# Delta rule with VectorE block transposes, eight slots to a loop turn, and a head start on the output projection

## The chip, the cores and the metric

The kernel runs on one core of one Trainium2 chip. The metric is the time of one execution on the device, in microseconds (us). TensorE, VectorE (DVE), ScalarE (ACT), GpSimd (POOL) and SyncE (SP) work through their own instruction streams and meet at semaphores.

## The reference

One decoder layer on x of 4 sequences by 512 tokens by 512 features, in float32:

```
x = x + attn(layernorm(x))      # gated delta rule, 16 key heads, 32 value heads of 128
x = x + xattn(layernorm(x), ctx)
x = x + ffn(layernorm(x))
```

The change touches the first line only. Its attention is

```
mixed = silu(causal_conv(h @ w_qkv, 4 taps)); q, k, v = split(mixed); q, k = l2norm(q), l2norm(k)
per token: S = S*exp(g); delta = (v - k.S)*beta; S = S + k x delta; o = q.S
core = rmsnorm(o) * norm_weight * silu(h @ w_z);  out = core @ w_out      # 4096 -> 512
```

## The kernel before

A first stage writes the normalized x, turned, into SBUF (`xT`, 128 x 4 x 2048). `delta_rule` then goes through 64 units, one for each of 16 key heads (with its two value heads) and 4 sequences. `tail` does the output projection, the cross attention and the feed-forward part.

The delta rule is a pipeline of **slots**. Slot n projects and prepares unit n (`project`), inverts the triangular matrices of unit n-1 (`invert`) and runs the recurrence of unit n-2 (`recur`), in four chunks of 128 tokens. Each engine has its own order of the pieces of a slot, written out by hand in a function `slot` in its block, and every engine works strictly in that order. `slots` unrolls the first `ROUND` = 4 slots, then a hardware loop (`Fori(1, ROUNDS, 1)`, 15 turns of 4 slots) runs the bulk, and two further slots drain the pipeline: slot 64 with invert and recur, slot 65 with recur alone. In the trace, line 618 is the projection (`tile(n, j)`, 4 matrix products of 128x512 f32, each of which is two MATMUL records), six of them to a slot.

**The inversion.** For each of 2 heads and 4 chunks a 128x128 unit triangular matrix is inverted by doubling, in float16. The blocks grow from 2x2 (`LEVELS` = 6 levels, block half `2 << l`). Two copies are kept: `dm`, the inverse so far, and `em`, its transpose. A level l makes z = (B times even columns of dm), masked by VectorE into `zm` (line 923); d = em times zm, which VectorE adds into `dm` (line 927); and e = zm times odd columns of em, which VectorE adds into `em` (line 933). On TensorE these are `level_z` (line 688), `level_d` (697) and `level_e` (708), 8 products of 128x64 f16 each. `em` starts as the masked matrix plus identity, made by GpSimd (`e_masked`, line 538, `e_first`, line 544). Its transpose is made by TensorE (`turn_e0`, line 677, products with a float16 identity, 4 for each head) and copied by ScalarE (`copy_d0`, line 1128).

**The recurrence** is a chain through all four engines: `solve` (747), ScalarE copies `uu` (1144), `grow` (755), `attend` (766), VectorE updates the state (957), `read_k` (730), VectorE makes the residual (947), `solve` again. At its end GpSimd scales the outputs (564, 566, 573), TensorE turns them (`o_turn`, 772), VectorE gates them (`gated`, 973), and SP stores them to `core_rows` in HBM.

**The tail** opens with the output projection: for each of 16 token tiles, 32 products of 128x512 f32 (`project_out`, line 1384), one for each value head, accumulated in four PSUM banks `acc`. The core comes back from HBM in pieces of four heads by four tiles (1 MB, SP queue, line 1315), the weights `wout` in four pieces of 2, 6, 12 and 12 heads, all issued at once from ScalarE's queue (line 1825).

Of the kernel before, what the change touches and what calls it, by code (L numbers as in the profile page):

```python
# [23 lines left out]
ROUND = 4  # L24
# [11 lines left out]
HC = FF // P  # L36

# [254 lines left out]
def delta_rule(nc, xT, tabs, cons, nw, decay_dram, w_dram, core_dram):  # L292

    with ExitStack() as ctx:
# [19 lines left out]
        id16 = sb("id16", [P, P], F16)  # L314
# [3 lines left out]
        junk = sb("junk", [P, 4 * NC, P], BF16)  # L318
# [3 lines left out]
        ring = [ctx.enter_context(nc.psum_tensor(f"d_ring{i}", [P, S], F32)) for i in range(RING)]  # L322
        tz, td, te = (ctx.enter_context(nc.psum_tensor(f"d_{n}", [P, S], F32)) for n in ("tz", "td", "te"))
# [12 lines left out]
        e0_ready, a_done, d0_ready = sem("e0_ready"), sem("a_done"), sem("d0_ready")  # L336
# [7 lines left out]
        def slots(eng, slot):  # L344

            for r in range(ROUND):
                slot((0, r), True, r >= 1, r >= 2)
            with eng.Fori(1, ROUNDS, 1) as q:
                for r in range(ROUND):
                    slot((q, r), True, True, True)  # L350
            slot((ROUNDS, 0), False, True, True)
            slot((ROUNDS, 1), False, False, True)

# [40 lines left out]
        def per_token(ap):  # L394
# [5 lines left out]
        RING_ORDER = ("k", "q", "v1", "k_turn", "v0_turn", "z1", "khat_turn",  # L400
                      "v1_turn", "kk", "kq", "v0", "z0", "q_turn")
        RING_BANK = {"k": 1, "q": 0, "v1": 2, "k_turn": 1, "v0_turn": 0, "z1": 0, "khat_turn": 0, "v1_turn": 1, "kk": 0, "kq": 2, "v0": 1, "z0": 2, "q_turn": 0}
        RING_FREED = {"k": (taps, "taps", 2), "q": (taps, "taps", 5), "v0": (taps, "taps", 8), "v1": (taps, "taps", 11),
                      "z0": (z_silued, "z_silued", 0), "z1": (z_silued, "z_silued", 1),
                      "k_turn": (khat_ready, "once", 0), "khat_turn": (kT_ready, "once", 0), "q_turn": (q_squares, "squares", NC - 1),
                      "kk": (bf_ready, "bf_ready", 1), "kq": (p_ready, "p_ready", 0),
                      "v0_turn": (vn_ready, "vn_ready", 0), "v1_turn": (vn_ready, "vn_ready", 1)}
        CONV_ORDER = ("k", "q", "v1", "v0")
        CONV_BUFFER = {name: i % 2 for i, name in enumerate(CONV_ORDER)}
        SILUED = {"k": (silued, "silued", 0), "q": (silued, "silued", 1), "v0": (silued, "silued", 2), "v1": (silued, "silued", 3)}  # L410
        POSITION = {"once": (1,), "squares": (1, 2, 3, 4), "projected": (1, 2, 4, 3), "tap0": (1, 2, 4, 3), "silued": (1, 2, 4, 3),
                    "taps": (1, 2, 3, 4, 5, 6, 10, 11, 12, 7, 8, 9), "e0_ready": (3, 1, 4, 2), "z_projected": (2, 1),
                    "z_silued": (2, 1), "gam_ready": (1, 2), "gamc_ready": (1, 2), "gams_ready": (2, 1), "ks_ready": (2, 1),
                    "bf_ready": (1, 2), "bh_ready": (2, 1), "bl_ready": (1, 2), "p_ready": (2, 1), "v_turned": (1, 2),
                    "vn_ready": (1, 2), "a_done": (2, 1), "d0_ready": (2, 1), "refined": (1, 2), "zr_ready": (1, 2),
                    "closed": (1, 2), "tt_ready": (2, 1), "o_turned": (1, 2), "core_ready": (1, 2)}
        LAGGED = ("z0", "z1", "kq", "v0_turn", "v1_turn")
# [8 lines left out]
        def free(eng, n, name, order, place, freed):  # L426

            slot_, v = back(n, -(name in LAGGED)), order.index(name)
            for _ in range(3 * len(order)):
# [4 lines left out]
                unit = back(slot_, order[v] in LAGGED)  # L434
# [6 lines left out]
        def _(sp):  # L441
# [12 lines left out]
            for j in (0, TILES, 1, 3, 2, 5, 4):  # L454
                load_weights(0, j)
# [33 lines left out]
            for r in range(ROUND):  # L489
                slot((ROUNDS - 1, r), True, True, True)  # L490
            slot((ROUNDS, 0), False, True, True)
            slot((ROUNDS, 1), False, False, True)
# [3 lines left out]
        def _(pool):  # L496

            nc.gpsimd.tensor_copy(id16[:, :], cons[:, C_ID:C_ID + P]).then_inc(ids_ready, 1)
# [10 lines left out]
            def k_norm(n):  # L509
# [3 lines left out]
                wait(pool, khat_ready, count(n, 1))  # L513
# [35 lines left out]

            def decayed_keys(m, h):  # L550
                pool.wait_ge(khat_ready, count(m))
                nc.gpsimd.tensor_tensor(by_chunk(ks_[m[1] % 2][h]), by_chunk(khat[m[1] % 2]), per_token(tab(m, Q_BEND, h)),
                                        ALU.mult).then_inc(ks_ready, 1)
# [21 lines left out]
            def slot(n, project, invert, recur):  # L575
# [4 lines left out]
                if invert:  # L580
                    decayed_keys(m, 1)
                    decayed_keys(m, 0)
                if project:
# [4 lines left out]
                if invert:  # L588
                    i_minus_d(m, 0)
                if recur:  # L590
                    o_norm(s)
                    o_scale(s)
                if invert:
                    i_minus_d(m, 1)
                if project:
                    e_masked(n, 1)
                    e_first(n, 1)
                    q_norm(n)
                    e_masked(n, 0)
                    e_first(n, 0)  # L600
                    b_low(n, 0)
                    b_low(n, 1)

# [3 lines left out]
        def _(pe):  # L607
            def ring_free(n, name):
                free(pe, n, name, RING_ORDER, RING_BANK, RING_FREED)
# [27 lines left out]
            def khat_turn(n):  # L637
                pe.wait_ge(khat_ready, count(n))
# [29 lines left out]
            def turn_e0(m, h):  # L668
                if first(m):
                    pe.wait_ge(ids_ready, 1)  # L670
                pe.wait_ge(e0_ready, nth(m, "e0_ready", GV + h))
                if h == 0:
                    wait(pe, tt_ready, nth(m, "tt_ready", 1, 1))
                else:
                    wait(pe, zr_ready, nth(m, "zr_ready", 1, 1))
                for c in range(NC):
                    last = nc.tensor.matmul(chunk((tz, td)[h], c), piece(em[m[1] % 2], h, c), id16[:, :], start=True, stop=True)
                last.then_inc(a_done, 1)

            def level_z(m, l):  # L680
                if l == 0:
                    pe.wait_ge(d0_ready, at(m, GV, GV))
# [9 lines left out]
            def level_d(m, l):  # L692
                pe.wait_ge(z_ready, at(m, LEVELS, l + 1))
                if l:
                    pe.wait_ge(e_added, at(m, LEVELS, l))
# [5 lines left out]
            def level_e(m, l):  # L701
                pe.wait_ge(z_ready, at(m, LEVELS, l + 1))
                if l:
                    pe.wait_ge(e_added, at(m, LEVELS, l))
                else:
                    wait(pe, tt_ready, nth(m, "tt_ready", 0, 1))
# [14 lines left out]
            def close(m, h):  # L721
                pe.wait_ge(zr_ready, nth(m, "zr_ready", 0) if h == 0 else at(m, GV, GV))
                pe.wait_ge(e_added, at(m, LEVELS, LEVELS))
# [3 lines left out]

            def read_k(s, c):
                pe.wait_ge(s_ready, at(s, 6, 2 * c))
                nc.tensor.matmul(psa[:, 0:GV * P], chunk(kT[s[1] % 4], c), state[:, :], start=True, stop=True).then_inc(ks_s, 1)  # L730

            def read_q(s, c):
                pe.wait_ge(s_ready, at(s, 6, 2 * c))
                pe.wait_ge(o_ready, at(s, NC, c))
# [39 lines left out]

            def slot(n, project, invert, recur):
                m, s = back(n, 1), back(n, 2)
                if invert:
                    turn_e0(m, 1)
                if project:
                    tile(n, 0)  # L780
                if recur:
                    solve(s, 0)
                if invert:
                    turn_e0(m, 0)
                if project:
                    tile(n, 1)
                if invert:
                    level_z(m, 0)
                if recur:
                    grow(s, 0)  # L790
                    attend(s, 0)
                if invert:
                    level_d(m, 0)
                    level_e(m, 0)
                if recur:
                    read_k(s, 1)
                if project:
                    tile(n, 3)
                if invert:
                    level_z(m, 1)  # L800
                if recur:
                    solve(s, 1)
                    read_q(s, 1)
                if project:
                    k_turn(n)
                if invert:
# [1168 lines left out]
```

## Time and profile before

| | |
|---|---|
| median of 3 runs | 3666.68 us (3666.51 to 3670.01) |
| the profiled execution | 3667.28 us, of which the span of the trace is 3665.5 us |
| TensorE busy, mean granted clock | 3487.7 us (95%), 0.977 |
| VectorE, ScalarE, GpSimd busy | 2314.8 (63%), 1369.4 (37%), 1520.7 us (41%) |
| delta rule, from its first product to the last store | about 105 to 2806 us |
| tail | about 2806 us to the end |

The span is cut by stages: what holds in one does not hold in another. In the timeline a row is start, duration, engine, line, operation, output and inputs, shape, count, and in brackets the idle time of the engine before it with what ended it. TensorE's products are pipelined: a product's duration includes its latency, so costs on TensorE are read from the distance between starts.

### The profile page before, as it was taken

The page shows a single profiled execution, that of the slowest core. Times are in us where ns is not written, and L with a number is a line of the kernel's source. Part 1 is how long each engine was busy: PE and PEld are TensorE (multiplying, and loading weights), DVE is VectorE, ACT ScalarE, POOL GpSimd, SP SyncE. Part 2 cuts the span into 40 slices and gives each one's busy share as a digit, 9 for nine tenths or more (in the row PEclk, how much of TensorE's full clock was granted, in tenths as well). Part 3 has the DMA queues.
Part 4 walks back from the last instruction along what each step waited for, and adds up shares of the span by engine and source line. Part 5 has one row for each costly group of instructions (what it writes and reads, how often), then busy time and mean ns, then how long its engine had stood idle before and what let it go on. Part 6 is the DMA issues. An engine that isn't in the chain of part 4 may idle for free. (4 is left out here: it accounts for less than half of the span.)

```text
span 3665.5 us, 67720 instructions
## 1 busy us (share of the span) xinstructions
PE 3487.7 (95%) x23472; PEld 2207.6 (60%) x23472; DVE 2314.8 (63%) x4006; ACT 1369.4 (37%) x4187; POOL 1520.7 (41%) x1473
## 2 busy tenths in 40 slices
PE   4799999999999999999999999999996999999999
PEld 4466666666666666666666666666664444455444
DVE  4587777877778777878778777778772000014453
ACT  1344444444444444444444444444441000011232
POOL 0455554555545455555554555545551000001032
PEclk7999999999999999999999999999997999999999
DMA  1111111111111111111121111111104232311001
GB/s 55 44 36 30 42 42 37 30 36 44 34 36 30 36 32 51 30 36 36 31 48 30 36 30 41 43 37 30 36 24 157 87 115 69 103 58 69 1 9 38
DMA packets 94404, 165.88 MB, mean 45 GB/s; under 512 B 7841, under 2 KB 40737, under 8 KB 92449
## 3 DMA queue, kind: packets, MB, share of 16 engines
q1 hardware_dynamic: 93440, 152.47, 14.4%
q10 hardware_dynamic: 576, 8.39, 0.6%
q8 instruction: 225, 3.69, 0.4%
q14 instruction: 163, 1.33, 0.1%
HBM read 122.83 MB, written 38.01 MB: 44 GB/s over the span
## 5 line engine op out<-in xcount | busy, mean ns | idle before, releaser
L618 PE MATMUL d_ring<-xT,d_w 128*128 128x512 f32 x3072 | 1424.5, 607 | 12.0 <-DMA d_w<-in_w 11.6
L618 PEld LDWEIGHTS d_ring<-xT,d_w 128*128 128x128 f32 x3072 | 574.7, 194 | 585.6 <-issue 567.2
L890 DVE SCALAR_TENSOR_TENSOR d_conv<-d_ring,d_w,d_conv 128x511 f32<-128x511 f32 (+2 forms) x768 | 570.7, 743 | 287.2 <-ACT d_conv L1082 282.4
L1384 PE MATMUL t_acc<-t_area 128*128 128x512 f32 x1024 | 444.8, 595 | 18.4 <-DMA t_area<-core_rows 18.4
L1082 ACT ACTIVATE d_conv<-d_ring,d_w 128x512 f32<-128x512 f32 x256 | 176.5, 689 | 599.3 <-PE d_ring L618 599.3
L1384 PEld LDWEIGHTS t_acc<-t_area 128*128 128x128 f32 x1024 | 194.5, 191 | 256.7 <-issue 237.9
L923 DVE TENSOR_TENSOR d_zm<-d_tz,cons 128x512 f16<-128x512 f32 x384 | 264.2, 688 | 118.9 <-PE d_tz L688 114.5
L559 POOL TENSOR_TENSOR d_imd<-cons,d_dm 128x512 f16<-128x512 f32 x128 | 148.4, 1160 | 434.5 <-ACT d_dm L1133 434.5
L1613 DVE TENSOR_TENSOR t_x<-t_acc,t_x 128x512 f32<-128x512 f32 x16 | 11.1, 692 | 419.5 <-PE t_acc L1384 419.5
L511 POOL TENSOR_TENSOR d_rkt<-d_kss,cons 128x4 f32<-128x4 f32 x64 | 12.9, 201 | 610.9 <-ACT d_junk L1100 610.9
L933 DVE TENSOR_TENSOR d_em<-d_te,d_em 128x512 f16<-128x512 f32 x384 | 262.1, 683 | 4.5 <-PE d_td L697 0.2
L1873 POOL TENSOR_SCALAR t_veps<-t_mv 128x1 f32<-128x1 f32 x32 | 9.7, 303 | 575.1 <-DVE t_mv L1623 575.1
L927 DVE TENSOR_TENSOR d_dm<-d_td,d_dm 128x512 f16<-128x512 f32 x256 | 175.7, 686 | 71.6 <-PE d_td L697 71.6
L1144 ACT ACTIVATE d_uu<-d_psa 128x256 f32<-128x256 f32 x256 | 98.2, 384 | 276.9 <-PE d_psa L747 276.9
L688 PEld LDWEIGHTS d_tz<-d_dm,d_bh 128*128 128x128 f16 x3072 | 138.5, 98 | 93.0 <-issue 72.1
L1148 ACT ACTIVATE d_junk<-d_oo 128x128 bf16<-128x128 f32 x512 | 154.8, 302 | 100.6 <-DVE d_oo L967 98.1
L544 POOL TENSOR_TENSOR d_em<-d_em,cons 128x512 f16<-128x512 f16 x128 | 186.9, 1460 | 10.0
L899 DVE TENSOR_TENSOR_SCAN d_gam<-d_decay,d_ident 128x512 f32<-128x512 f32 x128 | 170.2, 1330 | 24.9 <-issue 22.0
L520 POOL TENSOR_TENSOR d_gamc<-d_gam,d_tabm 128x512 f32<-128x512 f32 x128 | 164.0, 1282 | 20.5 <-POOL d_tabm L507 13.7
L1775 ACT ACTIVATE t_xT<-t_turn 128x512 f32<-128x512 f32 x32 | 18.2, 596 | 397.2 <-PE t_turn L1367 397.2
L766 PE MATMUL d_psb<-d_uu,d_pT 128*128 128x128 f32 x1024 | 162.8, 282 | 0.6 <-ACT d_uu L1144 0.5
L525 POOL TENSOR_TENSOR d_gam<-d_gamc,cons 128x512 f32<-128x512 f32 x128 | 159.9, 1271 | 5.0
(223 smaller groups left out, 6791.1 us busy)
## 6 DMA issues: line engine op xcount, KB each, us to landing
d_decay<-decay_rows SPq DMA_DIRECT2D x64, 512.0 KB, 6.1
core_rows<-d_core SPq DMA_DIRECT2D x64, 512.0 KB, 3.3
t_area<-core_rows SPq DMA_DIRECT2D x32, 1024.0 KB, 5.5
d_w<-in_w SPq DMA_DIRECT2D x96, 256.0 KB, 2.8
t_area<-in_wout ACTq DMA_DIRECT2D x2, 3072.0 KB, 21.3
ln_x<-in_x SPq DMA_DIRECT2D x16, 256.0 KB, 5.1
t_x<-in_x SPq DMA_DIRECT2D x4, 1024.0 KB, 9.9
t_area<-in_ctx SPq DMA_DIRECT2D x4, 1024.0 KB, 7.5
```

The source lines that it names most:

```text
L520: nc.gpsimd.tensor_tensor(by_chunk(gamc[n[1] % 2][h]), by_chunk(gam[h]), per_token(tab(n, Q_BETA, h)), ALU.mult).then_inc(gamc_ready, 1)
L525: nc.gpsimd.tensor_tensor(by_chunk(gam[h]), by_chunk(gamc[n[1] % 2][h]), bc(cons[:, C_LT:C_LT + P], NC), ALU.mult).then_inc(gams_ready, 1)
L544: nc.gpsimd.tensor_tensor(e0, e0, bc(cons[:, C_ID:C_ID + P], NC), ALU.add).then_inc(e0_ready, 1)
L618: last = nc.tensor.matmul(bank(TILE[j])[:, :], wtile(j, k), xT[:, k, r % B * S:(r % B + 1) * S], start=k == 0, stop=k == KT - 1)
L766: last = nc.tensor.matmul(chunk(psb, h), chunk(pT[s[1] % 2][h], c), chunk(uu, h), start=True, stop=True)
L890: nc.vector.scalar_tensor_tensor(c[:, d:S], bank(TILE[j])[:, 0:S - d], tap(j, KS - 1 - d), c[:, d:S], ALU.mult, ALU.add).then_inc(taps, 1)
L899: nc.vector.tensor_tensor_scan(gam[h][:, :], decay[r % 2][:, h, :], ident[:, :], 0.0, ALU.mult, ALU.add).then_inc(gam_ready, 1)
L923: nc.vector.tensor_tensor(even(zm[l], l), packed(tz, l), bc(mask, GV * NC), ALU.mult).then_inc(z_ready, 1)
L927: nc.vector.tensor_tensor(even(dm, l), packed(td, l), even(dm, l), ALU.add).then_inc(d_added, 1)
L933: nc.vector.tensor_tensor(odd(e, l), packed(te, l), odd(e, l), ALU.add).then_inc(e_added, 1)
L1082: nc.scalar.activation(conv_of(TILE[j])[:, :], bank(TILE[j])[:, :], ACT.Copy, scale=tap(j, KS - 1)).then_inc(tap0, 1)
L1384: return nc.tensor.matmul(acc[t][:, :], core[(grp * CHUNKS + q) % 3][:, t, h * P:(h + 1) * P], w[:, head, :], start=head == 0, stop=head = ...
```

## The change

1. `turn_e0` and `copy_d0` go. VectorE makes the transpose itself: `flip_e0` transposes `em` in 32x32 blocks into `dm` (one instruction, 128x1024 f16).
2. `level_e` goes for levels 0 to 3 on TensorE and VectorE. `flip_d(m, l)` transposes `dm` back into `em` in 32x32 blocks after each `level_d` of levels 0 to 3 (up to level 3 nothing lies outside diagonal blocks of 32). Levels 4 and 5 stay as they were, `level_d` of level 5 and `level_e` of 4 and 5 on TensorE.
3. `normal_k`, `first_state` and the first `output` move from VectorE to ScalarE. `p_full`, twice a slot, moves from VectorE to GpSimd, which can't read PSUM, so ScalarE copies the product first (`copy_kq`).
4. The order of the pieces of a slot is new on all four engines, and so are the banks and buffers given to them.
5. `ROUND` goes from 4 to 8: 8 slots unrolled ahead, 7 turns of 8 slots.
6. During slots 64 and 65 SP loads the cores of heads 0 to 7 of the first sequence and their weights into `xT` (4 transfers of 1 MB). 24 of the output projection's products are spread over slot 65 on TensorE, between the steps of the recurrence. The tail does the other 8 of these first, starts its own loads at head 8, and issues the second to fourth piece of weights one by one, each when a piece of the core has landed.

```diff
-ROUND = 4
+ROUND = 8
+EARLY = 24
...
-            def turn_e0(m, h):
...
-                    last = nc.tensor.matmul(chunk((tz, td)[h], c), piece(em[m[1] % 2], h, c), id16[:, :], start=True, stop=True)
...
+            def flip_e0(m):
+                dve.wait_ge(e0_ready, at(m, 2 * GV, 2 * GV))
+                nc.vector.transpose(dm[:, :], em[m[1] % 2][:, :]).then_inc(flipped, 1)
+
+            def flip_d(m, l):
+                dve.wait_ge(d_added, at(m, 4, l + 1))
+                nc.vector.transpose(em[m[1] % 2][:, :], dm[:, :]).then_inc(flipped, 1)
...
+            def p_full(m, h):
+                pool.wait_ge(kqs_ready, count(m))
+                pool.wait_ge(gamc_ready, nth(m, "gamc_ready", h))
+                nc.gpsimd.tensor_tensor(pT[m[1] % 2][h][:, :], kqs[:, :], gamc[m[1] % 2][h][:, :], ALU.mult).then_inc(p_ready, 1)
...
+            def head_start(n, i):
+                if isinstance(n[0], int) and n == (ROUNDS, 1):
+                    if i == 0:
+                        pe.wait_ge(early[0], 48)
+                        pe.wait_ge(vn_ready, GV * ITERS)
+                        pe.wait_ge(z_silued, GV * ITERS)
+                        pe.wait_ge(zr_ready, GV * ITERS)
+                    for piece in range(EARLY * i // 19, EARLY * (i + 1) // 19):
+                        if piece == 4 * KT:
+                            pe.wait_ge(early[1], 16)
+                        early_product(nc, acc, xT, piece)
...
+            sp.wait_ge(z_projected, GV * (ITERS - 1))
+            sp.wait_ge(stored, 16 * (ITERS - 4))
+            for q, b in ((0, 1), (1, 0)):
+                sp.dma_start(xT[:, :, b * S:(b + 1) * S], core_rows[0:NC, :, q * S:(q + 1) * S].rearrange("t p n -> p t n")).then_inc(early[0], 16)
+            sp.dma_start(xT[:, :, 2 * S:3 * S], wout[:, 0:KT, :]).then_inc(early[0], 16)
...
-        PARTS = (0, 2, 8, 20, HV)
+        PARTS = (8, 12, 16, 24, HV)
...
+            for piece in range(EARLY, 8 * KT):
+                early_product(nc, acc, xT, piece)
...
             for i in range(4):
+                if i:
+                    act.wait_ge(core_loaded[i - 1], 16)
```

The new order on TensorE in one slot (n: project, m: invert, s: recur; `flip` stands for the VectorE transpose that it waits for):

```
tile(n,0) | z0 (after flip_e0) | solve0 | kq | d0 | grow0 attend0 | z1 | read_k1 | tile(n,1) | solve1 |
d1 (after flip_d 0) | k_turn | read_q1 grow1 | z2 | tile(m,5) | d2 | attend1 read_k2 | khat_turn | z3 |
read_q2 solve2 | kk | grow2 | d3 | tile(n,2) | z4 | attend2 read_k3 | d4 e4 | read_q3 | q_turn | solve3 |
z5 | v_turn1 | attend3 | d5 e5 | tile(n,3) | refine x2 | tile(m,4) | close0 | o_turn x2 | close1 | v_turn0
```

VectorE's new slot begins `flip_e0, decays, level_z(0), convolve, level_d(0), convolve, level_z(1)`.

## Rows read from the trace of the kernel before

**Rows 1.** Windows: a steady slot; the last slot with the drain after it.

```profile
core 0: us, PE busy (x) PEld busy (x) DVE busy (x) ACT busy (x) POOL busy (x), PEclk, DMA share, GB/s
1125.30:1165.43 40.13, 40.13 (x327) 27.53 (x325) 32.13 (x57) 19.36 (x64) 22.42 (x21) 1.00 0.11 32
...
2778.20:2806.50 28.30, 15.19 (x64) 10.64 (x64) 7.51 (x19) 6.07 (x26) 3.73 (x3) 0.73 0.11 38
```

**Rows 2.** Timeline of TensorE: first products of slots 1, 2 and 64.

```profile
134.44 0.38 PE L677 MATMUL d_td<-d_id,d_em 128*128 128x128 f16 x4 [3.43 <-POOL d_em L544]
...
170.48 0.39 PE L677 MATMUL d_td<-d_id,d_em 128*128 128x128 f16 x4
...
2744.18 0.39 PE L677 MATMUL d_td<-d_id,d_em 128*128 128x128 f16 x4
```

**Rows 3.** Timeline of TensorE: removed pieces and what starts behind them.

```profile
1007.56 0.40 PE L708 MATMUL d_te<-d_em,d_zm 128*128 128x64 f16 x8
1007.80 0.68 PE L730 MATMUL d_psa<-d_state,d_kT 128*128 128x256 f32 x2
...
1042.53 0.39 PE L677 MATMUL d_tz<-d_id,d_em 128*128 128x128 f16 x4
1042.76 2.79 PE L618 MATMUL d_ring<-xT,d_w 128*128 128x512 f32 x6
```

**Rows 4.** Timeline of TensorE: the start of a loop turn.

```profile
1082.15 0.60 PE L677 MATMUL d_td<-d_id,d_em 128*128 128x128 f16 x4 [3.48 <-POOL d_em L544]
1082.55 6.48 PE L618 MATMUL d_ring<-xT,d_w 128*128 128x512 f32 x8
1088.87 0.61 PE L747 MATMUL d_psa<-d_vn,d_tt 128*128 128x128 f32 x4
```

**Rows 5.** Groups of instructions by line and shape: VectorE.

```profile
L933 DVE TENSOR_TENSOR d_em<-d_te,d_em 128x512 f16<-128x512 f32 x384 | 262.1, 683 | 4.5 <-PE d_td L697 0.2
...
L952 DVE COPY d_state<-d_psa 128x256 f32<-128x256 f32 x64 | 26.5, 415 | 2.5 <-PE d_psa L755 2.5
...
L1685 DVE SCALAR_TENSOR_TENSOR t_area<-t_area,t_thr 128x1024 f16<-128x1024 f32 x1 | 1.3, 1285 | 0.0
...
L1684 DVE TENSOR_SCALAR t_area<-t_area,t_nthr 128x1024 f16<-128x1024 f32 x1 | 0.8, 755 | 0.0
...
L899 DVE TENSOR_TENSOR_SCAN d_gam<-d_decay,d_ident 128x512 f32<-128x512 f32 x128 | 170.2, 1330 | 24.9 <-issue 22.0 <-DMA d_decay<-decay_rows 2.9
...
L263 DVE RECIPROCAL gt_be<-gt_w 128x512 f32<-128x512 f32 x1 | 3.4, 3354 | 0.0
```

**Rows 6.** Groups of instructions by line: GpSimd and ScalarE.

```profile
L525 POOL TENSOR_TENSOR d_gam<-d_gamc,cons 128x512 f32<-128x512 f32 x128 | 159.9, 1271 | 5.0
...
L1137 ACT ACTIVATE d_oq<-d_psb,d_tabm 128x128 f32<-128x128 f32 x384 | 118.8, 362 | 15.4 <-PE d_psb L735 15.2
...
L1128 ACT ACTIVATE d_dm<-d_td 128x512 f16<-128x512 f32 x64 | 38.2, 597 | 49.7 <-PE d_td L677 49.7
```

**Rows 7.** Timelines of TensorE and VectorE: from level_z to level_d of level 0.

```profile
1006.11 0.40 PE L688 MATMUL d_tz<-d_dm,d_bh 128*128 128x64 f16 x8
...
1007.32 0.40 PE L697 MATMUL d_td<-d_zm,d_em 128*128 128x64 f16 x8
...
1006.55 0.69 DVE L923 TENSOR_TENSOR d_zm<-d_tz,cons 128x512 f16<-128x512 f32 x1 [0.95 <-PE d_tz L688]
```

**Rows 8.** Timeline of TensorE: slot 65 and the first product of the tail.

```profile
2779.10 0.71 PE L747 MATMUL d_psa<-d_vn,d_tt 128*128 128x128 f32 x4 [2.11 <-DVE d_tt L943]
...
2794.21 0.71 PE L766 MATMUL d_psb<-d_uu,d_pT 128*128 128x128 f32 x4 [0.47 <-ACT d_uu L1144]
2800.43 1.12 PE L772 MATMUL d_psa<-cons,d_oo 128*128 128x128 f32 x4 [5.50 <-POOL d_oo L573]
...
2820.79 9.52 PE L1384 MATMUL t_acc<-t_area 128*128 128x512 f32 x16 [18.40 <-DMA t_area<-core_rows]
```

**Rows 9.** The chain that ended last, in order of time: start, us, what.

```profile
2806.53 14.22 DMA t_area<-core_rows
2820.79 30.12 PE t_acc L1384 x64
...
2865.98 96.14 PE t_acc L1384 x224
```

More of the change, by code:

```diff
@@ L352, in slots, with long_slots @@
             slot((ROUNDS, 1), False, False, True)
+        def long_slots(eng, slot):
+            for r in range(ROUND):
+                slot((0, r), True, r >= 1, r >= 2, r >= 3)
+            with eng.Fori(1, ROUNDS, 1) as q:
+                for r in range(ROUND):
+                    slot((q, r), True, True, True, True)
+            slot((ROUNDS, 0), False, True, True, True)
+            slot((ROUNDS, 1), False, False, True, True)
+            slot((ROUNDS, 2), False, False, False, True)
         def count(n, before=0):
@@ L666, in _ @@
             PIECES = [(h, c) for h in range(GV) for c in range(NC)]
-            def turn_e0(m, h):
[L669 to L676, printed above, removed]
-                    last = nc.tensor.matmul(chunk((tz, td)[h], c), piece(em[m[1] % 2], h, c), id16[:, :], start=True, stop=True)
-                last.then_inc(a_done, 1)
             def level_z(m, l):
                 if l == 0:
-                    pe.wait_ge(d0_ready, at(m, GV, GV))
+                    pe.wait_ge(flipped, at(m, 5, 1))
+                    wait(pe, tt_ready, nth(m, "tt_ready", 1, 1))
                 elif l < 5:
@@ L693, in level_d @@
                 pe.wait_ge(z_ready, at(m, LEVELS, l + 1))
[L694 to L695 removed]
+                if l == 0:
+                    wait(pe, zr_ready, nth(m, "zr_ready", 1, 1))
+                elif l < 5:
+                    pe.wait_ge(flipped, at(m, 5, l + 1))
+                else:
+                    pe.wait_ge(e_added, at(m, 2, 1))
                 for h, c in PIECES:
@@ L789, in slot @@
                 if recur:
+                    solve(s, 0)
+                    head_start(n, 0)
+                if invert:
+                    kq(m)
+                    level_d(m, 0)
+                if recur:
                     grow(s, 0)
+                    head_start(n, 1)
                     attend(s, 0)
[L792 to L798, printed above, removed]
+                    head_start(n, 2)
                 if invert:
@@ L871, in slot @@
                 if recur:
+                    solve(s, 3)
+                    head_start(n, 15)
+                if invert:
+                    level_z(m, 5)
+                    v_turn(m, 1)
+                if recur:
+                    attend(s, 3)
+                    head_start(n, 16)
+                if invert:
+                    level_d(m, 5)
+                    level_e(m, 5)
+                if project:
+                    tile(n, 3)
+                if invert:
+                    refine(m, 1)
+                    refine(m, 0)
+                    tile(m, 4)
+                    close(m, 0)
+                if recur:
+                    o_turn(s, 0)
+                    head_start(n, 17)
                     o_turn(s, 1)
+                    head_start(n, 18)
                 if invert:
-                    close(m, 0)
                     close(m, 1)
+                    v_turn(m, 0)
             slots(pe, slot)
```

461 lines of the change are left out of this document (233 added, 228 removed).

## The prediction, made before the changed kernel ran

> **What bounds the kernel now.** I read the table of engines first (TensorE busy 95%), then cut the span into stretches. In a steady slot TensorE is busy for all 40.13 us, at full clock [rows 1]. VectorE is busy for 32.1 of them, GpSimd for 22.4, ScalarE for 19.4. So in the delta rule TensorE's own work is the time. A cut there counts whole, and work put on the others is free as long as they keep up. Three things are not steady. At the back edge of the loop TensorE idles 3.5 us and its next eight products take 6.48 us [rows 4]. The last slot is a chain of small steps with TensorE busy for 15.2 of 28.3 us and a granted clock of 0.73 [rows 1]. The tail opens with 14.2 us of waiting for transfers [rows 9]. Behind that the chain that ended last is nearly all TensorE again.
>
> **Removed from TensorE.** A `level_e` holds it for 1007.80 - 1007.56 = 0.24 us, a `turn_e0` for 1042.76 - 1042.53 = 0.23 us [rows 3]. The other removed ones differ by 0.01. Four of the first and two of the second make 1.39 us a slot, for 64 slots with inversion 89.0 us. The steady slot goes from 40.14 to 38.75 us if nothing new holds TensorE up.
>
> **Do the others keep up?** VectorE loses four `level_e`, two `p_full` and `normal_k`, all of the 128x512 form at 0.683 us, and two copies of 0.415 us [rows 5]: 5.61 us. It gains five block transposes of 128x1024 f16. The trace shows none. From below: the 128x1024 operation in the fastest mode seen takes 0.755 us; from above: a scan of 512 takes 1.33, so 2.66 us for 1024 [rows 5]. I take 1.285 us, the row of one element at a time over the same 1024 elements. Then VectorE has 32.1 - 5.6 + 6.4 = 32.9 us in a slot of 38.75, 85%. With the lower bound it has 30.3, with the upper 39.8 us. The Trainium skill (VectorE: DVE Perf Modes, The three transpose paths) gives 311 ns for 128x128 bf16 in 32x32 blocks. An estimate from it, 896 further elements at its 0.96 GHz, is 1.24 us each and would leave the sum where it is; no row here shows a transpose.
>
> GpSimd gains two `p_full`, at 1.27 us as its nearest row [rows 6]: 22.4 + 2.5 = 25.0 us. ScalarE loses two copies of 0.597, gains one of them back as `copy_kq`, four of 128x128 at 0.362 for `normal_k` and two of 128x256, at most 0.6 each [rows 6]: 19.4 + 2.1 = 21.5 us. Both have room.
>
> Totals don't show waits inside the slot, so I walked through the new order by hand. From the start of `level_z` to that of `level_d` at least 1.21 us pass (products, 0.44 to the mask, 0.69 the mask) [rows 7]. In the new order `solve0` and `kq` stand between z0 and d0, about 0.9 us, and 0.24 of z0: a hole of 0.07. Between d0 and z1 stand `grow0` and `attend0`, about 1 us, while VectorE puts a tap of the convolution ahead of the addition: a hole of 0.1 to 0.2. Everywhere else a projection tile (3.4 us) or several small pieces cover the flip and the addition. `flip_e0` runs under `tile(n,0)` with about 1 us to spare; if it is late, z0 is, and with it the whole level 0. I put 0.2 us a slot: +12.8 us, with bounds of 0 and 0.5 (0 and 32 us).
>
> **The loop.** From slot 2 to slot 64 are 62 slots, 2573.7 us [rows 2], 85.3 more than 62 times 40.135. There are 14 back edges, so one costs 6.1 us: about 3.3 idle and 2.8 for products at half clock (6.48 where 3.65 is usual) [rows 4]. With eight slots there are 6 back edges: 8 times 6.1 = -48.8 us. At a turn TensorE now meets a tile first, but the idle stretch is its own restart, and I leave its price.
>
> **The start.** In slot 0 TensorE waited 3.43 us for GpSimd's `em` [rows 2]. Now `tile(1,0)` stands in front of the first use: -3.4 us.
>
> **Slots 64 and 65 and the opening of the tail.** A product of the output projection costs 96.14 / 112 = 0.86 us (224 records, two each) [rows 9]. 24 of them leave the tail: -20.6 us. The tail's first load wait, 14.2 us [rows 9], is filled by the 8 further products, 6.9 us at full clock and some 2.8 more if the clock has dropped, while 2 MB come in instead of all pieces at once: -14.2 us. In exchange slot 65 fills up. From `solve0` to `attend3` it took 2794.21 - 2779.10 = 15.1 us [rows 8]. There are 20 products in that stretch now, 17.2 us, beside 7.5 us of its own products at full clock (0.43 to 0.52 each). One or two products cover each step of ScalarE or VectorE, so it is their sum, 24.7: +9.6 us. The 5.5 us for GpSimd before `o_turn` [rows 8] stay, and the last four products lie under it and under the store. I add 2.8 us for one more half-clock stretch, as a turn of the loop shows. Together -22.4 us. The early loads wait in SP's queue ahead of the store of slot 64. What they wait for (projections and older stores) is long done, or, for the last one, done some microseconds before, and no compute waits behind them. In slot 64 with few tiles the chain of levels sets the time, and two VectorE steps of a level (1.3 us) become three (2.6 us), one of them beside the products: +1.5 us.
>
> **Sum**, against the profiled execution's 3667.28 us (0.6 above the median): 3667.3 - 89.0 + 12.8 - 48.8 - 3.4 - 22.4 + 1.5 = 3518 us. With no holes and no half clock in slot 65 it is 3501, with 0.5 us of holes 3537.
>
> **Rivals.**
> (a) *The flips are as dear as a scan.* At 2.66 us VectorE has 39.8 us of work a slot and becomes the bound; slots of 39.8 to 40.3 us instead of 38.95 give 3572 to 3604 us. For it: an instruction no row prices. Against: it has one input and no carried sum.
> (b) *A turn costs in proportion to its body.* 6 turns of 12.2 instead of 6.1 us: 3518 + 36.6 = 3555 us. For it: the body to fetch is twice as long. Against: once restarted, no stretch of a slot shows TensorE short of instructions.
> (c) *VectorE and GpSimd block each other.* A scan beside GpSimd takes 1.33 us in the mean, and GpSimd now reads SBUF for two more instructions. If each flip waits half of a 1.27 us instruction in the 64% of the time that GpSimd works, VectorE has 2 us more, 35 of 38.75, and the two tight places grow by some 0.6 us: +38 us, 3556 us. The Trainium skill (SBUF — State Buffer, Who interferes with whom) says that the two share one port pair, taken by a VectorE instruction with two SBUF inputs or in a two-port mode, and not by one with a single input outside these. By it a flip would stay clear unless it runs in a two-port mode; the trace can't say.
> (d) *The head start is void*: early data come late or the drain grows by as much as the tail loses. 3518 + 22 = 3540 us.
> (e) *Slower than before.* Outside the steady slot the change wins about 70 us, 1.1 us a slot. The slot must exceed 41.2 us for a loss, so flips must exceed (41.2 - 26.5) / 5 = 2.9 us. At the reciprocal's rate, 3.354 us for 512 elements [rows 5], 6.7 each, a slot would take 60 us and the kernel 3667 + 64 x 19.9 - 70 = 4870; at 3.5 us, 44.0 and 3844 us.
>
> **How the numbers follow.** The forecast 0.66, (a) 0.10, (b) 0.10, (c) 0.06, (d) 0.05, (e) 0.03. The range 3490 to 3580 holds the forecast, (b), (c), (d) and the cheap end of (a). The forecast's own is 3497 to 3540. A difference of over 0.2%, 7 us, is what can be told here: all but (e) are faster, and a little is kept for a dear flip between (a) and (e): faster 0.95, same 0.01, slower 0.04.
>
> **What would show it.** Flips of 1.1 to 1.4 us; steady slots of 38.75 to 39.3 us with TensorE busy throughout; 6 stretches of about 3.3 us idle with a half-clock tile behind; `solve0` to `attend3` of slot 65 in 25 to 28 us; no wait over 2 us in the tail's first 50 us. It is wrong if VectorE is busy over 95% in a slot, if TensorE waits on `flipped`, or if a turn costs over 9 us.

## The result, and the profile after

The changed kernel takes 3484.94 us (median of 4 runs, 3484.55 to 3488.6) where the kernel before takes 3667.24 on the same chip: a ratio of 0.9504, with a 95% interval from 0.9487 to 0.952. The gain is 182 us. I had forecast 149 and put the time between 3490 and 3580, so the sign and most of the mechanism came out and the size did not: the result lies 5 us under the range. The profiled execution of the change took 3488.6 us, with a span of 3485.6, against 3665.5 before.

The page of the changed kernel: the table of engines, then one group of instructions (busy us, mean ns of one, idle before).

```profile
PE 3369.7 (97%) x20912; PEld 2098.0 (60%) x20912; DVE 2352.2 (67%) x3750; ACT 1447.7 (42%) x4507; POOL 1646.7 (47%) x1600
...
L958 DVE STREAM_TRANSPOSE d_em<-d_dm 128x1024 f16<-128x1024 f16 x256 | 317.5, 1240 | 4.4
```

A flip takes 1.24 us. The windows of the changed kernel answer to [rows 1], first a steady slot, then from the first solve of slot 65 to the first product of the tail.

```profile
1071.12:1109.83 38.71, 38.71 (x291) 26.00 (x287) 32.88 (x52) 20.54 (x68) 24.38 (x23) 1.00 0.09 29
2624.40:2662.38 37.98, 31.72 (x112) 18.29 (x112) 5.82 (x15) 6.50 (x28) 3.73 (x3) 0.91 0.17 56
```

TensorE is still busy for the whole of a slot at full clock, and VectorE for 32.9 us of it (the forecast had 32.9). TensorE remains the bound, and what was cut from it counts whole. The drain of slot 65 has TensorE busy for 31.7 of 38.0 us.

The start of a turn on TensorE, which answers to [rows 4], and then on VectorE:

```profile
1024.00 0.61 PE L650 MATMUL acc<-cons,d_vraw 128*128 128x128 f32 x4
1027.08 5.39 PE L644 MATMUL acc<-xT,d_w 128*128 128x512 f32 x8 [2.48 <-issue]
```

```profile
1025.02 0.68 DVE L985 TENSOR_TENSOR d_tt<-d_tz,d_em 128x512 f32<-128x512 f32 x1
1027.52 1.25 DVE L954 STREAM_TRANSPOSE d_dm<-d_em 128x1024 f16<-128x1024 f16 x1 [1.82 <-issue]
```

TensorE idles 2.48 us here, and its tile runs in 5.39 us. At two of the six turns it idles 1.90 us and the tile takes 3.69, the time at full clock; these turns cost 2.1 us each. At the other four it idles 2.13 to 2.52, the granted clock is at half for part of the tile, which takes 5.39, and they cost 4.1 to 4.4. Before it idled 2.92 to 3.60 us.

The tail's opening on TensorE, which answers to the load wait of [rows 9]:

```profile
2654.54 1.12 PE L801 MATMUL d_psa<-cons,d_oo 128*128 128x128 f32 x4 [4.35 <-POOL d_oo L596]
...
2662.42 8.80 PE L1290 MATMUL acc<-xT 128*128 128x512 f32 x16 [1.96 <-PEq L295]
2671.06 19.48 PE L1452 MATMUL acc<-t_area 128*128 128x512 f32 x45
```

The eight further products take 8.80 us, and the first product that needs the large load starts right behind them, without a wait.

**Where the 180 us of span went**, by the time of the first solve of each slot:

| stretch | forecast | measured |
|---|---|---|
| start to the first solve of slot 2 | -4.6 (-3.4 for the wait, -1.2 for slot 1) | +1.8 |
| steady slots between 2 and 63 (61 of them) | -72 | -91 |
| turns of the loop in the same stretch | -49 | -63 |
| slots 63 and 64 | -1 | -2 |
| slot 65 and the tail | -22.4 | -25.2 (+10.6 and -35.8) |

A steady slot went from 40.14 us to 38.57 or 38.64, with 38.89 in every eighth. Fourteen turns cost 6.0 us each beyond a steady slot (84 us in all), six turns now cost 3.6 each (21 us). In the last row the first number runs from the first solve of slot 65 to the start of the tail (before 2806.5, in the change 2662.4), the second from there to the end.

### The profile page after: what moved, and what is told of

It reads as the page before. It is cut to its first block and busy times, and to the rows that moved or that the text cites. A ratio compares the mean times of both kernels' runs of the same rounds, so it can differ in the third digit from the quotient of the medians.

```text
span 3485.6 us, 61745 instructions
## 1 busy us (share of the span) xinstructions
PE 3369.7 (97%) x20912; PEld 2098.0 (60%) x20912; DVE 2352.2 (67%) x3750; ACT 1447.7 (42%) x4507; POOL 1646.7 (47%) x1600
## 5 line engine op out<-in xcount | busy, mean ns | idle before, releaser
L644 PE MATMUL acc<-xT,d_w 128*128 128x512 f32 x3072 | 1412.8, 603 | 25.4 <-issue 13.2
L644 PEld LDWEIGHTS acc<-xT,d_w 128*128 128x128 f32 x3072 | 563.1, 192 | 589.8 <-issue 573.9
L935 DVE SCALAR_TENSOR_TENSOR d_conv<-acc,d_w,d_conv 128x511 f32<-128x511 f32 (+2 forms) x768 | 570.2, 742 | 22.3 <-ACT d_conv L1114 16.1
L1452 PE MATMUL acc<-t_area 128*128 128x512 f32 x768 | 332.4, 592 | 0.0
L958 DVE STREAM_TRANSPOSE d_em<-d_dm 128x1024 f16<-128x1024 f16 x256 | 317.5, 1240 | 4.4
L1114 ACT ACTIVATE d_conv<-acc,d_w 128x512 f32<-128x512 f32 x256 | 177.6, 694 | 289.6 <-PE acc L644 289.6
L969 DVE TENSOR_TENSOR d_dm<-acc,d_dm 128x512 f16<-128x512 f32 x256 | 176.6, 690 | 105.1 <-PE acc L716 104.4
L550 POOL TENSOR_TENSOR d_bl<-d_bf,d_bh 128x512 f16<-128x512 f32 x128 | 148.1, 1157 | 167.9 <-ACT d_bh L1154 167.9
L571 POOL TENSOR_TENSOR d_pT<-d_kqs,d_gamc 128x512 f32<-128x512 f32 x128 | 163.0, 1274 | 5.4 <-ACT d_kqs L1170 5.4
L703 PE MATMUL d_tz<-d_dm,d_bh 128*128 128x64 f16 x3072 | 153.1, 193 | 6.6 <-DVE d_dm L954 4.4
```

Source lines behind the costliest of these rows:

```text
L571: nc.gpsimd.tensor_tensor(pT[m[1] % 2][h][:, :], kqs[:, :], gamc[m[1] % 2][h][:, :], ALU.mult).then_inc(p_ready, 1)
L644: last = nc.tensor.matmul(bank(TILE[j])[:, :], wtile(j, k), xT[:, k, r % B * S:(r % B + 1) * S], start=k == 0, stop=k == KT - 1)
L703: last = nc.tensor.matmul(packed(tz, l, (h * NC + c) * HALF, HALF), chunk(bh[m[1] % 2][h], c), even(dm, l, (h * NC + c) * P, P), start=Tru ...
L935: nc.vector.scalar_tensor_tensor(c[:, d:S], bank(TILE[j])[:, 0:S - d], tap(j, KS - 1 - d), c[:, d:S], ALU.mult, ALU.add).then_inc(taps, 1)
L958: nc.vector.transpose(em[m[1] % 2][:, :], dm[:, :]).then_inc(flipped, 1)
L969: nc.vector.tensor_tensor(even(dm, l), packed(td, l), even(dm, l), ALU.add).then_inc(d_added, 1)
```

## The experiments

Thirteen kernels ran, each beside the kernel before. "The change" is the changed kernel. Where slots are given, they are from one first solve to the next in that kernel's own trace, and the cost of a turn is what a turn takes beyond steady slots. Not all ran on the same chip, so a few us between two of them are read from the ratios too.

**1. Eight slots to a turn, nothing else.**

```
-ROUND = 4        (kernel before)
+ROUND = 8
```

> The kernel before with eight slots to a turn of the loop and nothing else changed (6 back edges for 14). Theory Q (what a turn costs hangs on how much work TensorE still has queued behind its last wait when the loop turns; the body's length has no part): a turn keeps its 6.1 us, so 8 x 6.1 = 49 us less than before, 3618 us. Rival L (a turn is cheaper with a longer body, down to the 3.6 us seen in the changed kernel): 6 turns for 21.5 us in place of 85.3, 64 us less, 3603 us. Rival B (a turn costs in proportion to the body): no change.

Measured: 3614.03 us (3607.9 to 3620.05), ratio 0.9858 (0.9843 to 0.9873). Its turns cost 5.0 to 6.6 us, 6.3 in the mean, where the same kernel with four slots pays 6.0. A body twice as long costs 0.3 us more a turn and not twice as much, so rival (b) is out. The loop alone gives about 50 us, as forecast.

**2. The change with four slots to a turn.**

```
-ROUND = 8        (the change)
+ROUND = 4
```

> The changed kernel with four slots to a turn (14 back edges for 6). Theory Q: a turn keeps the 3.6 us it has in the changed kernel's order, 8 x 3.6 = 29 us more, 3514 us. Rival L: the shorter body brings back 6.1 us a turn, 14 x 6.1 - 21.5 = 64 us more, 3549 us. Idle of TensorE at a turn: Q 1.9 to 2.6 us as now, L 3.3.

Measured: 3542.9 us (3538.96 to 3549.36), ratio 0.9671. The time comes near rival L, but TensorE's idle stretch is that of theory Q, 2.0 to 2.4 us: neither had the cause. A turn costs 6.0 us in this form, not 3.6. VectorE shows why. The timeline of VectorE, then SyncE's queue in the same stretch:

```profile
1047.21 1.25 DVE L954 STREAM_TRANSPOSE d_dm<-d_em 128x1024 f16<-128x1024 f16 x1 [1.58 <-issue]
1053.23 1.23 DVE L944 TENSOR_TENSOR_SCAN d_gam<-d_decay,d_ident 128x512 f32<-128x512 f32 x1 [4.78 <-issue]
```

```profile
1045.20 0.41 SPq L492 DMA_DIRECT2D core_rows<-d_core  x1
1046.23 0.38 SPq L463 DMA_DIRECT2D d_decay<-decay_rows  x1
```

VectorE stops twice. The second stop, ahead of its second instruction, comes in all of the 14 turns (4.25 to 5.62 us) and in none with eight slots. No semaphore holds it: the scan reads decays that were loaded a slot earlier. But it starts 7.0 us after SyncE issued the next decay load (512 KB to 128 partitions, 6.1 us from issue to landing in the median), so just when that load is in. This made two theories, tested next.

The profile's DMA view of a window also lists packets of the kind "instruction", which carry code. From 1051.30 to 1052.20, between the flip and the scan, it has (packets, MB, share of the 16 DMA engines):

```profile
q14 instruction: 2, 0.02, 6.0%
```

In all 14 turns two such packets of 8 KB start 3.5 to 4.6 us after the flip has started, and the scan starts 1.1 to 1.7 us after both have landed.

**3. That decay load later.** In the first slot of a turn SyncE now waits for the first projection tile of the gate z (`tile(m,5)`, called `z1` in the code) in mid-slot, and issues the load some 17 us after its old place.

```
 if project and not (...last unit...):
+    if r == 0 and not first(n):
+        sp.wait_ge(z_projected, at(back(n, 1), GV, 1))
     load_decay((q, r + 1))
```

> The changed kernel with four slots to a turn; in the first slot of a turn the 512 KB load of the next slot's decays is issued by SyncE some 15 us later (after the tile of z in the middle of the slot), nothing else is changed. With four slots VectorE stops twice in each turn, the second time for 4.3 to 5.6 us ahead of its second instruction, and in the trace that instruction starts 0.9 to 1.0 us after the decay load, issued just after the turn, has landed. Theory T (the second stop is VectorE fetching instructions, and that fetch shares the DMA engines with the 512 KB load, so it ends when the load ends): the second stop shrinks to under 3 us, a turn costs about 3.6 to 4.5 us instead of 5.7, and the time falls from 3543 to 3512 to 3527. Theory C (the fetch itself takes that long at this place of the code, load or no load): the second stop stays above 4 us, 3540 to 3546.

Measured: 3502.32 us (3500.02 to 3504.5), ratio 0.9555 (0.9541 to 0.957): 41 us less than in experiment 2. VectorE at the same turn:

```profile
1033.56 1.25 DVE L956 STREAM_TRANSPOSE d_dm<-d_em 128x1024 f16<-128x1024 f16 x1 [1.72 <-issue]
1036.26 1.22 DVE L946 TENSOR_TENSOR_SCAN d_gam<-d_decay,d_ident 128x512 f32<-128x512 f32 x1 [1.45 <-issue]
```

The second stop is still there, but takes 1.3 to 1.8 us. The two code packets now start 0.6 to 0.9 us after the flip has, and the scan again follows the last of them by 1.1 to 1.7 us: with the load out of the way the code comes about 3 us sooner, and VectorE with it. A turn costs 2.9 us, less than I expected and less than in the change itself. That last difference is the clock: 13 of these 14 turns run TensorE's tile at full clock (2.7 us a turn), two of the change's six do (2.1 us a turn).

**4. VectorE's code shifted.**

```
 (VectorE, ahead of its first slot)
+for i in range(64):
+    nc.vector.memset(tt[0][0][:, 8 * i:8 * i + 8], 0.0)
```

> The changed kernel with four slots to a turn and 64 memsets of 8 columns more on VectorE, ahead of its first slot, when it idles for the first loads: they move the code of all slots by 64 instructions. They themselves cost nothing on the path. If the second stop of VectorE in each turn hangs on where the head of the turn lies in its code (it comes just where a piece of the stream ends that was not fetched yet), it moves or vanishes: the scan behind the first flip starts without the 4.3 to 5.6 us of idle time, a turn costs about 3.6 us, 3512 to 3520. If it is a matter of four slots' length alone, or of the load, it stays: 3540 to 3546.

Measured: 3506.33 us (3504.32 to 3512.28), ratio 0.9564. With the load in its old place and 64 instructions ahead of the loop, the second stop is gone:

```profile
1039.06 1.25 DVE L956 STREAM_TRANSPOSE d_dm<-d_em 128x1024 f16<-128x1024 f16 x1 [1.49 <-issue]
1040.23 1.18 DVE L946 TENSOR_TENSOR_SCAN d_gam<-d_decay,d_ident 128x512 f32<-128x512 f32 x1
```

Experiments 3 and 4 fit together. In each turn an engine has to bring in the code at the loop's head anew. Where the head lies just ahead of a border between two pieces of VectorE's code, it stops again there; that it is such a border is argued from the shift, not seen. And beside a 512 KB load the code packets come about 3 us later, and the second stop takes 4.3 to 5.6 us, without it 1.3 to 1.8. That they wait for the same DMA engines is argued from these times. Turns in experiment 4 cost 3.8 us; some have a second stop on TensorE in front of `level_z` (1.1 to 2.8 us).

**5. The same load later in the kernel before.** The edit of experiment 3, word for word, on the kernel before.

> The kernel before, with the 512 KB load of the next slot's decays issued some 15 us later in the first slot of each turn, as in the changed kernel with four slots; nothing else. Before, TensorE stops for 2.9 to 3.6 us at a turn and resumes some 1.9 us after that load was issued; in the change it stops for 1.9 to 2.5 us. If the load is what holds its instructions up (theory T), the first stop falls to 2 to 2.5 us, the second stops at the first solve (1.1 to 2.5 us, in some turns) go, half the clock's loss goes with them, and a turn costs 4 to 5 us instead of 6.1: 3640 to 3655. If the longer stop is of this kernel's own order (theory O), the first stops stay at 3 us and over and only the second ones go, 14 x 0.5 us at most: 3657 to 3668.

Measured: 3625.49 us (3623.15 to 3631.71), ratio 0.9901 (0.9886 to 0.9916). One wait on SyncE saves 36 us; the load comes some 23 us later here. The opening of a turn up to the first solve, then the tile of another turn, as windows of the kernel before:

```profile
1082.15:1088.87 6.72, 6.72 (x12) 3.06 (x13) 1.64 (x1) 0.60 (x1) 5.78 (x6) 0.55 0.22 78
748.55:752.63 4.08, 3.91 (x12) 1.65 (x12) 1.84 (x1) 0.65 (x2) 3.83 (x4) 1.00 0.77 136
```

and in this experiment (the last three numbers are the granted clock, the DMA engines' busy share and GB/s):

```profile
1073.99:1077.75 3.76, 3.75 (x13) 1.85 (x14) 1.77 (x1) 0.60 (x1) 3.51 (x5) 1.00 0.09 26
```

with TensorE there:

```profile
1073.99 0.40 PE L679 MATMUL d_td<-d_id,d_em 128*128 128x128 f16 x4 [2.92 <-POOL d_em L546]
1074.23 3.68 PE L620 MATMUL d_ring<-xT,d_w 128*128 128x512 f32 x8
1077.75 0.61 PE L749 MATMUL d_psa<-d_vn,d_tt 128*128 128x128 f32 x4
```

The first stop only falls from 2.9 to 3.6 us to 2.9 to 3.3 us, so this part went as theory O said. But the tile behind it runs in 3.68 us instead of 6.48, with a granted clock of 1.00 where it was 0.55, and the second stops at the first solve (1.1 to 2.5 us in 5 of the 14 turns) are gone. A turn costs 3.5 us instead of 6.0, which I had expected of neither theory in this size.

The clock is not what the load cost, though. Before, three of the 14 turns ran their tile at full clock, as the window from 748.55 shows, and still cost 5.9 us in the mean (the other 11: 6.1). TensorE in that turn:

```profile
748.78 3.68 PE L618 MATMUL d_ring<-xT,d_w 128*128 128x512 f32 x8
755.00 0.71 PE L747 MATMUL d_psa<-d_vn,d_tt 128*128 128x128 f32 x4 [2.53 <-issue]
```

and the code packet that moves from 752.40 to 753.60 in the same trace:

```profile
q8 instruction: 1, 0.02, 5.7%
```

Before, this packet (16 KB; by its times it is TensorE's) starts 2.6 to 4.5 us after TensorE has resumed, and in the nine turns in which TensorE idles ahead of the first solve, the solve starts 1.2 to 1.5 us after the packet has landed. With the load late the packet starts 0.3 to 0.5 us after the restart and no solve waits. So what the load costs here is late code again, and at half clock the slow tile only hides that wait. The half clock has a price of its own, 1.8 us: the two turns of this experiment that still have it cost 5.0 us in the mean, the other twelve 3.3. Why they are fewer with the load late is open: the length of the stop does not decide it, for in the change with four slots a stop of 2.04 us was followed by half clock and one of 2.32 by full.

**6. Sixteen slots to a turn.**

```
-ROUND = 8        (the change)
+ROUND = 16
```

> The changed kernel with sixteen slots to a turn: 2 back edges instead of 6, nothing else. If a turn costs the 3.6 us measured with eight slots, whatever the body's length (3.58 a turn in the change), the time falls by 4 x 3.6 = 14 us: 3469 to 3473. If a longer body makes a turn dearer in proportion (7.2 us at sixteen), the gain is 6 x 3.6 - 2 x 7.2 = 7 us: 3477 to 3479. If a second stop such as with four slots comes back on some engine, 4 us less: 3473 to 3475.

Measured: 3469.33 us (3466.55 to 3473.08), ratio 0.9467 (0.9454 to 0.948). 16 us less with four turns fewer; the two that are left cost 4.6 and 3.9 us, not the 7.2 of a price in proportion to the body.

**7. The last tile of a unit put at the end of TensorE's work in a turn.**

```
-tile(m, 4)
+if n[1] != ROUND - 1: tile(m, 4)
 ... refine, close(m, 0), o_turn, close(m, 1), v_turn ...
+if n[1] == ROUND - 1: tile(m, 4)
```

> The changed kernel, with the projection tile(m,4) moved behind v_turn as TensorE's last piece, in the last slot of each turn alone. Theory Q: 3.4 us of work queued behind the last wait cover most of the restart; idle at the turn falls from 1.9-2.5 us to under 1, the half-clock stretch goes, and 6 turns lose 2 to 3.6 us each, less what the pieces that the tile used to cover now wait (up to 1 us each): 3465 to 3480 us. Rival (the restart begins only when TensorE's last product is done): idle at the turn stays 1.9 to 2.5 us and the time 3485 to 3490.

Measured: 3485.64 us (3484.37 to 3486.9), ratio 0.9513: no gain, where theory Q wanted 5 to 20 us. Rows of TensorE:

```profile
1022.45 0.40 PE L745 MATMUL d_te<-d_em,d_zr 128*128 128x128 f16 x4 [1.59 <-DVE d_zr L983]
...
1024.53 7.03 PE L644 MATMUL acc<-xT,d_w 128*128 128x512 f32 x16
...
1034.52 0.71 PE L784 MATMUL d_psa<-d_uu,d_ks 128*128 128x128 f32 x4 [1.06 <-ACT d_uu L1189]
```

TensorE's stop at the turn is gone, 16 products run through it at full clock. But the tile used to hide the step from `refine` to `close`, which now waits 1.59 us, and ScalarE, which restarts 4.25 us late, holds up the products after it. Covering one engine's restart uncovers the next one's.

**8. Each of the four level flips done twice.**

```
 nc.vector.transpose(em[m[1] % 2][:, :], dm[:, :]).then_inc(flipped, 1)
+nc.vector.transpose(em[m[1] % 2][:, :], dm[:, :]).then_inc(again, 1)
+dve.wait_ge(again, at(m, 4, l + 1))
```

> The changed kernel with each of the four flips from dm to em done twice in a row (the second writes the same values again, and only it releases TensorE). VectorE goes from 32.9 to 38.0-38.3 us a slot of 38.6. This puts a price on the forecast's rival (a), flips at 2.5 us. Theory: the room is there in sum and not where it is needed; slots of 39.6 to 41 us, 60 to 150 us more, 3545 to 3635 us. Rival (idle time of VectorE takes it in): slots under 38.8, less than 15 us more.

Measured: 3637.86 us (3636.61 to 3639.97), ratio 0.9929. Slots take 41.1 to 41.2 us, 2.5 more, for 5 us more of VectorE's work. So even with only four of the five flips at 2.5 us the kernel takes 153 us more, just over the range that I expected, and not the 54 to 86 of rival (a): the rival was rightly placed and priced too low. VectorE was busy for 37.5 of 41.1 us, so it was not full; TensorE waited 1.3 us of that slot for two masks (`zm`) that VectorE made late.

**9. No head start, and a longer one.** `EARLY = 0` and `EARLY = 32` in place of 24.

> The changed kernel without products in slot 65 (EARLY = 0); the early loads stay, and the tail begins with all 32 of the products that they feed. Theory: the tail gets 24 x 0.859 = 20.6 us longer and slot 65 some 9 to 11 us shorter: 10 to 12 us more than the changed kernel, 3495 to 3497 us; so of the 25 us won at the end of the delta rule the larger part came from opening the tail on data that are there, not from the products between the steps. Rival (all of the 20.6 us were won): 3506 us.

> The changed kernel with all 32 products in slot 65 (EARLY = 32). Theory: 8 products, 8.8 us, leave the opening of the tail, where they covered the first loads; there TensorE now waits 6 to 8 us for them, and slot 65 grows by 3 to 6 us: 0 to 6 us more than the changed kernel, 3485 to 3491. Rival (loads are not what the 8 products cover): 3 to 5 us less.

Measured: 3494.84 us (3494.0 to 3495.89), ratio 0.9539, and 3492.05 us (3489.37 to 3496.12), ratio 0.9534. With none, the 32 products run behind slot 65 in 30.27 us: the 24 products inside the slot are worth 10 us by the times and 13 by the ratios. With 32 the time lies 1 us over the range that I had expected. With 32, none is left for the tail, and its first product meets the load again:

```profile
2669.96 20.44 PE L1452 MATMUL acc<-t_area 128*128 128x512 f32 x41 [10.19 <-DMA t_area<-core_rows]
```

**10. Both closing products side by side.**

```
 close(m, 0)
+close(m, 1)
 ... o_turn twice ...
-close(m, 1)
 v_turn(m, 0)
```

> The changed kernel with close(m,1) moved up beside close(m,0), ahead of the two o_turns: one switch from float16 to float32 products fewer in each slot, same work. Theory S (a float32 product costs 0.08 us more behind a float16 one, which is why the removed pieces gave 1.56 us a slot and not 1.39): slots of 38.48 to 38.56 for 38.57 to 38.64, 64 x 0.08 = 5 us less, 3480 us. Rival (order of types is free): 3485 us, unless a wait shows: a later o_turn costs nothing.

Measured: 3481.79 us (3481.64 to 3485.38), ratio 0.9506 (0.9493 to 0.9519), which can't be told from the change. Slots are 38.56 and 38.63 us instead of 38.57 and 38.64: a switch from 128-column f16 to f32 products costs nothing here. This corrected my reading of the slot, below.

**11. Sixteen slots with the edit of 10, and then with that of 3 as well.**

> Sixteen slots to a turn, and both closing products of a unit beside each other (one switch from f16 to f32 products less in each slot, which gave 3.2 us by itself). If the two add: 14 + 3 us below the change, 3465 to 3470.

> Sixteen slots to a turn, the closing products side by side, and the decay load late in the first slot of a turn. Without the last edit its two turns cost 7.0 and 4.7 us, and in the first TensorE stopped a second time for 2.8 us in the middle of its tile. Theory T: both turns fall to 2.5 to 4 us, 3463 to 3467. If the load has nothing to do with it: 3468 to 3471.

Measured: 3470.05 us (3468.05 to 3470.78) and 3467.22 us (3465.39 to 3471.53), ratios 0.9465 and 0.9467. All three kernels with sixteen slots are the same by this measurement. The two turns cost 7.0 and 4.7 us in the first and 4.4 and 6.2 in the second, where I had expected 2.5 to 4. In all six turns of the three kernels TensorE stops a second time, in the middle of its tile; the first turn of the kernel with the edit of 10:

```profile
1330.32 2.41 PE L644 MATMUL acc<-xT,d_w 128*128 128x512 f32 x5 [2.12 <-issue]
1335.52 2.72 PE L644 MATMUL acc<-xT,d_w 128*128 128x512 f32 x3 [2.79 <-issue]
```

The sixth of the tile's eight records starts 1.4 to 3.4 us after the fifth, where 0.43 is usual at full clock, and 1.0 to 1.4 us after a 16 KB code packet has landed. With the load late it is still 1.7 and 1.8 us, so here the load is not what makes the turns dear; the code is late without it. These are two turns of one execution each. The best kernel of the study is the change with sixteen slots, 5.3% faster than before.

## Why the prediction was right in kind and short in size

The steps that failed are two terms of the sum: the price of the turns that are left, and what a steady slot saves. I took 6.1 us for each of the six turns and they cost 3.6; I took 38.95 us for a slot and it is 38.66. Together they hold the 31 us by which the span fell more than forecast, and the paragraphs on the slot and the turns say what was measured in their place.

**VectorE flips.** Right, and the largest risk of the forecast: 1230 to 1246 ns a flip, inside the 1.1 to 1.4 us forecast. Rival (a) and the losing rival (e) fell with it. Rival (c) fell too: no flip is stretched beyond 1.25 us although GpSimd works in 63% of a slot. The Trainium skill (SBUF — State Buffer, Who interferes with whom) says of a VectorE instruction with one SBUF input, outside the two-port modes, that it stays clear of GpSimd; these durations agree. The forecast's estimate of 1.24 us from the Trainium skill (VectorE: DVE Perf Modes, The three transpose paths) was met by the mean, 1.24.

**The steady slot** (forecast 38.95, measured 38.66 in the mean, 18 us in all). Two steps failed. The first is the term for holes, 0.2 us a slot: there are 0 to 0.07, and 0.3 in every eighth slot. The second is that I priced only the removed products. The same f32 group costs 0.52 us behind a 64-column f16 group and 0.44 behind anything else; rows of the kernel before, each group's start to the next one's:

```profile
1138.80 0.40 PE L688 MATMUL d_tz<-d_dm,d_bh 128*128 128x64 f16 x8
1139.04 0.69 PE L747 MATMUL d_psa<-d_rr,d_tt 128*128 128x128 f32 x4
1139.57 0.60 PE L735 MATMUL d_psb<-d_state,d_qT 128*128 128x256 f32 x2
1140.00 0.60 PE L624 MATMUL d_ring<-cons,d_kraw 128*128 128x128 f32 x4
```

and of the change:

```profile
1077.93 0.61 PE L776 MATMUL d_psa<-d_rr,d_tt 128*128 128x128 f32 x4
1078.37 0.40 PE L716 MATMUL acc<-d_zm,d_em 128*128 128x64 f16 x8
```

The solve takes 0.53 us behind a level product and 0.44 behind a tile. A slot had 11 groups in such a place and has 9 now, so 2 x 0.08 = 0.16 us more is gone than the removed 1.39. From these rows I first blamed any switch of type; experiment 10, which removes one behind a 128-column group and gains 0.01 us a slot, speaks for the 64-column groups only. That the two missing places give the 0.16 us is argued from the rows, not run by itself.

**The turns** (forecast -48.8, measured -63, 14 us). The count was right: eight back edges fewer, 48 us (experiment 1, with the same eight fewer, gained 50), and no price in proportion to the body's length. The failed step is "at a turn TensorE now meets a tile first, but the idle stretch is its own restart, and I leave its price". The six turns left cost 3.6 us, not 6.1. I had split the 6.1 into 3.3 us of idle time and 2.8 for products at half clock, from the rows of one turn. The second part was mostly something else. Before, TensorE's next piece of code came 2.6 to 4.5 us after the restart, behind a 512 KB load, and the first solve could not start until it was in; the turns with a tile at full clock cost as much as the others (experiment 5). With the load late, a turn costs 3.5 us before and 2.9 in the change with four slots. In the change with eight slots the same load is in flight, issued 0.2 to 1.0 us before TensorE resumes instead of 1.4 to 2.4, but the code packet starts 0.8 to 2.3 us after the restart, and TensorE does not stop for it. What is left is the first stop, 1.9 to 2.5 us, and in four of the six turns 1.7 us for the tile at half clock. Whether a late load would lower these turns too was not tried with eight slots. Why TensorE's own stop is 1.9 to 2.5 us in the change and 2.9 to 3.3 before, even without the load, was not tried either; the code at the head of the turn differs in place and in content.

**The start** (forecast -3.4 for the wait and -1.2 for slot 1, measured +1.8). The wait of 3.43 us for `em` did go from TensorE's record, but the chain through `em` stayed: it has a flip in it now, and the wait moved behind the tile.

```profile
140.76 0.41 PE L703 MATMUL d_tz<-d_dm,d_bh 128*128 128x64 f16 x8 [2.14 <-DVE d_dm L954]
```

In slot 0 nothing is queued that could hide it. The delta rule also began 1.4 us later in this execution (first `d_w` load). In the ten other kernels with the same start the first solve of slot 2 comes at 172.3 to 174.8 us, and at 174.2 before: the change wins nothing there, and most of the 1.8 is of this execution.

**Slot 65 and the tail** (forecast -22.4, measured -25.2). The mechanism held step by step: `solve0` to `attend3` takes 24.3 us (24.7 forecast), the wait for GpSimd stays (4.35 us), the load wait is gone, and experiment 9 shows both sides of it: without the products in slot 65 10 to 13 us are lost, and with all 32 products inside the slot the load wait is back at 10.2 us. Rival (d) would have needed 22 us.

**The chances.** 0.66 for the likeliest case was fair for its mechanism. Its own range, 3497 to 3540, reached down only as far as no holes and no half clock in slot 65 (3502 by the terms, where the text has 3501), and took in nothing for the turn, though its two parts (idle, half clock) had no shown cause.

## What to carry to other kernels

When a loop's turn costs several microseconds, look at what DMAs are issued just after it, and in the DMA view at when the code packets move. A large prefetch moved some 23 us later gave 36 us in the kernel before, and one moved 17 us gave 41 us in the change with four slots, for one wait on SyncE. A slow tile behind a stop can hide a second wait: look for the turns that ran at full clock and see whether they were cheaper. When products are removed, price also what the neighbours pay: start to start of the next group, before and after. And of two parts of a cost whose cause isn't shown, forecast each with a range of its own, downwards too.

## What the hardware showed that I had not expected

A restart of VectorE at the loop's head can hang on where the code lies: 64 memsets ahead of the loop took a second stop of 4.3 to 5.6 us out of every turn, and 36 us from the kernel. An engine's stop for its own code stands in the timeline only as idle time before "issue", or under the name of a releaser that had long been done (`em` by GpSimd at TensorE's turns before). The DMA view shows the other half: packets of the kind "instruction", 16 KB or 8 KB each, and an engine that stopped for them goes on 1.0 to 1.7 us after they have landed.

A transpose of 128x1024 f16 within blocks takes 1.23 to 1.25 us on VectorE in all 320 cases, with GpSimd busy in 63% of a slot.
